# The bias of q, k and v in matmul rows that a column parity leaves empty, and the convolution's columns ordered by phase before channel

## The chip, the cores and the metric

The kernel runs on 1 core of one Trainium2 chip. The metric is the device time of one launch in microseconds (us). Before the change the median of 3 runs is 811.29 us (810.05 to 811.31). The core has TensorE (PE in the profile; PEld is its weight load), VectorE (DVE), ScalarE (ACT), GpSimd (POOL) and SyncE (SP), which here only issues DMAs.

## What is computed

The input x is (4, 32, 128, 128). Cut to what matters here:

```python
xw = group_norm(x) in windows of 16 x 16      # 64 windows an image
q = shuffle_invert(conv3(xw, qw, qb), 2)      # 3x3, 32 -> 32 channels, zero padding at the window's edge
k = shuffle_invert(conv3(xw, kw, kb), 2)      # a window's 16 x 16 pixels become 64 tokens
v = shuffle_invert(conv3(xw, vw, vb), 2)      # of 128 features: 32 channels x 2 x 2 phases
q, k, v = ln(q, gq, bq), ln(k, gk, bk), ln(v, gv, bv)
attn = softmax(q @ k.T * SCALE + bias[None])  # 8 heads of 16 features
out = (attn @ v) @ proj_w.T + proj_b          # back to pixels, plus xw: xr
y = xr + conv3(gelu(conv3(xr, c1w, c1b)), c2w, c2b)
return x + y
```

## The kernel before

Work is tiled by image (4), in an image by row of windows (8) and in a row by pair of windows (4): 32 pairs an image, 128 in all. One pair gives 128 tokens, the partitions of the result y_ps, which has 384 columns: 128 for q, 128 for k, 128 for v.

**The convolution of a pair** (PE, function step, lines 1010 and 1015) is one accumulation of 13 products in one bank. The input lies in SBUF as four copies shifted by one column: partition 32*col + channel, col 0 to 3. The free side is split by row parity, so one product covers one of four row offsets a (0 to 3) for both phases of the output. A phase (py, px) is the parity of the output pixel's row and column. Offset 0 is needed only by py = 0 and offset 3 only by py = 1, so these take half the columns (192). Input and weights are each a sum of two fp16 parts, high and low, and three products of them are taken: x_hi w_hi, x_hi w_lo, x_lo w_hi. The tokens' side is the stationary operand, the weights are streamed. Ahead of the twelve stands the bias product (line 1010): rows of ones (ones_b) against the bias split into three bf16 parts in b_parts. Since kx = col - px, columns of px = 0 have zero weights in rows 96 to 127 (col 3), and columns of px = 1 in rows 0 to 31 (col 0).

**Column order.** In each of q, k, v the 128 columns run over (py, head, channel in head, px). Normalising (ScalarE, line 855 for q and k, line 863 for v) reads them into the order (head, py, channel and px), so in runs of 8.

**The pipeline.** step(i) runs on each engine for i from -5 to 36 in an image. In step i the pair i+5 is convolved, the pair i+3 transposed (line 1040), the pair i scored (line 1056), i-2 has its softmax result transposed (line 1069) and i-3 is multiplied by v (line 1081). Each engine goes through its list in the order written, and semaphores tie them. From step 28 on PE also does the tiles of the first late convolution (c1, line 982), and the steps -5 to 2 of the next image do the second (c2, line 1138). After pair i+5's convolution VectorE takes the layer norm's statistics (line 541), GpSimd makes scales of them (lines 726 to 738), ScalarE normalises. The convolution of pair m waits for ln_v of pair m-2, which empties its bank.

**A row of inputs.** SP loads the shifted rows into xs (row, line 310), ScalarE normalises them (line 785), VectorE zeroes the window's edge, ScalarE writes x_hi (line 793, two halves; for row r in steps 4r-9 and 4r-8) and GpSimd x_lo (line 708). The row's first convolution is in step 4r-5.

**SP's order** in an image: the loads of rows 4 to 7 (each waits until the row two before it is normalised), the eight loads of xf, the four of the next image's xst, the next image's rows 0 to 3, then eight stores, each of which waits for its result. Image 0's rows 0 to 3 and the constants come ahead.

**Start.** VectorE finds the largest weights, scales, splits the weights (line 393) and takes the group norm's statistics (line 450). GpSimd splits the bias in nine operations (lines 694 to 696) and then takes the group norm's inverse deviation (line 701), on which the first row's normalisation waits.

Of the kernel before, what the change touches and what calls it, by code (L numbers as in the profile page):

```python
# [8 lines left out]
F16 = mybir.dt.float16  # L9
BF16 = mybir.dt.bfloat16  # L10
# [5 lines left out]
P = 128  # L16
# [4 lines left out]
E = 4 * C  # L21
# [17 lines left out]
W_TOP = 16.0  # L39
F16_TOP = 60000.0  # L40
# [4 lines left out]
GQ, BQ, GK, BK, GV, BV, PB, C1B, EVEN, ODD, C2B, EVEN2, ODD2, WIN0, WIN1, GVP, GVP1, BVP, BVP1 = range(19)  # L45
NVEC = 19
# [8 lines left out]
def conv_attention(nc, x_al, x_sh, wqkv, bqkv, bias_t, proj_t, vecs, w1, w2, ident, sel_mean, sel_ones, out):  # L55
    with ExitStack() as ctx:
# [22 lines left out]
        ones_f = sb("ones_f", [P, P])  # L79
        ones_b = sb("ones_b", [P, P], BF16)  # L80
# [4 lines left out]
        b_parts = sb("b_parts", [P, QKV], BF16)  # L85
        b_tmp = sb("b_tmp", [P, QKV], BF16)
# [84 lines left out]
        bias_split = sem("bias_split")  # L171
        c_scaled = sem("c_scaled")
# [80 lines left out]
        def by_head(y):  # L253

            return y.rearrange("p (y h x) -> p h y x", y=2, h=HEADS)
# [34 lines left out]
        def _(sp):  # L290
# [3 lines left out]
            for dst, src in ((wst, wqkv), (vec, vecs), (idf, ident), (bst, bqkv), (ones_f, sel_ones),  # L294
                             (selm, sel_mean)):
                load(dst, src, loaded_qkv)
# [15 lines left out]

            def image(b, followed):
                for r in range(4, NROW):
                    row(b, r)
# [3 lines left out]
                if followed:  # L319

                    sp.wait_ge(xr_begun, b * 4 + 5)
                    load_image(b + 1)
                    for r in range(4):
                        row(b + 1, r)
                for t in range(T2N):
                    sp.wait_ge(y_ready, b * T2N + (t + 1) + 1)
                    sp.dma_start(out[b, :, 512 * t:512 * (t + 1)], xf[t][:, :]).then_inc(stored, 16)
# [6 lines left out]
            for r in range(2, 4):  # L334
                row(0, r)
# [4 lines left out]
        def _(v):  # L340
# [29 lines left out]
            v.wait_ge(loaded_qkv, 16 * 6)  # L370
# [5 lines left out]
            v.tensor_copy(ones_b[:, :], ones_f[:, :])  # L376
            spread(0, 0, A_PROJ)

            link(v.tensor_scalar(sw[:, :], amax_all[:, 0:3], 1e-15, None, ALU.max))
# [287 lines left out]
        def _(pool):  # L667
# [12 lines left out]
            pool.wait_ge(loaded_qkv, 16 * 6)  # L680
# [12 lines left out]
            for j in range(3):  # L693
                bias_link(pool.tensor_copy(b_tmp[:, :], bst[:, :]))
                bias_link(pool.tensor_copy(b_parts[32 * j:32 * j + 32, :], b_tmp[32 * j:32 * j + 32, :]))
                bias_link(pool.tensor_tensor(bst[:, :], bst[:, :], b_tmp[:, :], ALU.subtract))
# [74 lines left out]
        def _(act):  # L771
# [48 lines left out]
            def step(i, p0, h0, r0, rr0, row0, b=None, followed=False, last=None):  # L820
# [27 lines left out]
                if has(i + 5):  # L848
# [5 lines left out]
                    for t in range(2):  # L854
                        ins = act.activation(qk_n[j][:, t, :].rearrange("p (h y x) -> p h y x", h=HEADS, y=2),  # L855
# [6 lines left out]
                    for w in range(2):  # L862
                        ins = act.activation(  # L863
                            v_bd[m % 8][:, :, w, 0:2 * HD].rearrange("p h (a y x) -> p h a y x", a=2, y=2),
                            y_ps[j][:, 2 * E:3 * E].rearrange("p (y h a x) -> p h a y x", y=2, h=HP, a=2),
# [69 lines left out]
        def _(pe):  # L935
# [62 lines left out]
            def step(i, p0, h0, r0, rr0, row0, b=None, followed=False, last=None):  # L998

                if has(i + 5):  # L1000
# [9 lines left out]
                    pe.matmul(y, ones_b[0:96, :], b_parts[0:96, :], start=True, stop=False)  # L1010
                    for a in range(4):

                        cols = {0: slice(0, E // 2), 3: slice(E // 2, E)}.get(a, slice(0, E))
                        for xx, ww in ((x_hi, w_hi), (x_hi, w_lo), (x_lo, w_hi)):
                            ins = pe.matmul(y.rearrange("p (t e) -> p t e", t=3)[:, :, cols],  # L1015
                                            xx[r % 2][:, s, a % 2, 2 * TS * (a // 2):2 * TS * (a // 2 + TS)],
                                            ww[:, a, :].rearrange("p (t e) -> p t e", t=3)[:, :, cols],
# [259 lines left out]
```

## Time and profile before

| | us |
|---|---|
| median of 3 runs | 811.29 |
| the profiled execution's own time | 810.2 |
| its span | 808.4 |
| PE matmul busy | 744.3 |
| PE weight loads busy (overlap the matmuls) | 549.4 |
| VectorE busy | 657.2 |
| ScalarE busy | 569.1 |
| GpSimd busy | 491.9 |

TensorE's granted clock is at 0.9 of full speed or more in each fortieth of the span. Busy time counts the durations of instructions; matmuls overlap, so what one costs is read from the distance between starts. A wait is put down to the instruction that came last. The chain of waits is the path that ended last, followed back to the start. Times in the rows below count from the span's start.

### The profile page before, as it was taken

How to read it: one execution, taken by the hardware profiler on the slowest of the kernel's cores; microseconds unless marked ns; L12 is line 12 of the kernel's file. 1: busy time of each engine (PE TensorE's matmuls, PEld its weight loads, DVE VectorE, ACT ScalarE, POOL GpSimd, SP SyncE). 2: the span in 40 equal slices, each digit the busy share in tenths (PEclk: the TensorE clock that was granted, in tenths of full speed). 3: DMA queues.
4: the chain of work that ended last, by engine and by line, in shares of the span. 5: the costliest groups of instructions: out<-in, count | busy, mean ns of one | idle time of the engine just before them, and what ended most of it. 6: DMA issues, size and time to landing. Idle time of an engine off the chain costs nothing.

```text
span 808.4 us, 18167 instructions
## 1 busy us (share of the span) xinstructions
PE 744.3 (92%) x5898; PEld 549.4 (68%) x5898; DVE 657.2 (81%) x2150; ACT 569.1 (70%) x1191; POOL 491.9 (61%) x1041
## 2 busy tenths in 40 slices
PE   0469999999899999999899999999999999999988
PEld 0247877777556778877555778777655688787753
DVE  6549889897859899897967989899775989887675
ACT  1399888767367988876547978876737788878630
POOL 6368778741457788763346777874244778886210
PEclk9999999999999999999999999999999999999999
DMA  7112331000013161000101332100101314000002
GB/s 266 59 30 60 96 144 60 2 1 23 38 65 97 33 239 44 18 1 1 59 33 54 110 125 116 60 1 2 56 5 66 98 32 135 2 2 2 2 1 104
DMA packets 17662, 47.32 MB, mean 59 GB/s; under 512 B 2080, under 2 KB 2720, under 8 KB 17568
## 3 DMA queue, kind: packets, MB, share of 16 engines
q1 hardware_dynamic: 17568, 46.15, 16.7%
q8 instruction: 48, 0.79, 0.4%
q14 instruction: 46, 0.38, 0.1%
HBM read 37.76 MB, written 8.39 MB: 57 GB/s over the span
## 4 chain that ended last, share of the span: by engine, by line
PE 67%; DVE 12%; ACT 9%; issue 5%; POOL 5%; DMA 0%; SPq 0%; POOLq 0%; ACTq 0%; DVEq 0%
PE y_ps L1015 18%; PE o_bank L1081 9%; PE s_ps L1056 8%; PE pt_ps L1069 7%; PE y_ps L982 4%; PE s_ps L1097 3%; PE t_ps L1040 3%; PE ox_ps L1138 3%; PE o_bank L1138 3%; PE pt_ps L1138 3%; PE s_ps L1138 3%; PE y_ps L1010 2%; DVE h_lo L505 2%; DVE h_hi L502 2%; ACT qk_n L855 1%
## 5 line engine op out<-in xcount | busy, mean ns | idle before, releaser
L743 POOL TENSOR_TENSOR sc<-sc,mx 128x512 f32<-128x512 f32 x128 | 133.7, 1044 | 59.9 <-DVE mx L568 59.9
L855 ACT ACTIVATE qk_n<-y_ps,ln_nr,ln_rs 128x128 f32<-128x128 f32 x256 | 104.4, 464 | 88.4 <-POOL ln_nr L733 88.2
L1015 PE MATMUL y_ps<-w_hi,x_hi 128*128 128x192 f16 (+1 forms) x512 | 147.2, 287 | 0.0
L1015 PE MATMUL y_ps<-w_hi,x_lo 128*128 128x192 f16 (+1 forms) x512 | 146.9, 287 | 0.0
L1015 PE MATMUL y_ps<-w_lo,x_hi 128*128 128x192 f16 (+1 forms) x512 | 146.7, 287 | 0.0
L541 DVE BATCH_NORM_STATS2 ln_st<-y_ps 128x6 f32<-128x128 f32 x384 | 88.8, 287 | 60.1 <-PE y_ps L1015 58.9
L1081 PE MATMUL o_bank<-v_bd,pt 128*128 128x66 f32 x1024 | 129.1, 269 | 3.9 <-DVE on L589 3.8
L1081 PEld LDWEIGHTS o_bank<-v_bd,pt 128*128 128x128 f32 x1024 | 124.4, 192 | 5.5 <-DVE pt L575 4.7
L730 POOL TENSOR_TENSOR ln_rs<-ln_ve,neg_half 128x3 f32<-128x3 f32 x128 | 113.4, 886 | 10.7
L870 ACT ACTIVATE sc<-sc 128x512 f32<-128x512 f32 x128 | 82.8, 647 | 39.3 <-POOL sc L743 39.3
L863 ACT ACTIVATE v_bd<-y_ps,ln_vs 128x128 f32<-128x128 f32 x256 | 105.2, 475 | 0.0
L726 POOL TENSOR_TENSOR ln_ve<-ln_mv,eps_y 128x3 f32<-128x3 f32 x128 | 35.2, 275 | 105.6 <-DVE ln_mv L546 105.6
L561 DVE TENSOR_TENSOR sc<-s_ps,biasS 128x512 f32<-128x512 f32 x128 | 85.2, 666 | 16.6 <-PE s_ps L1056 16.5
L1056 PE MATMUL s_ps<-k_m,q_m 64*128 64x128 f32 x1024 | 91.6, 297 | 0.0
L568 DVE TENSOR_REDUCE mx<-sc 128x8 f32<-128x512 f32 x128 | 87.9, 686 | 4.4
L575 DVE COPY pt<-pt_ps 128x512 f32<-128x512 f32 x128 | 87.2, 681 | 2.8 <-PE pt_ps L1069 2.6
L715 POOL TENSOR_TENSOR xr_lo<-xr,xr_hi 128x512 f16<-128x512 f32 x32 | 36.2, 1131 | 86.8 <-ACT xr_hi L811 86.8
L1069 PE MATMUL pt_ps<-idf,sc 128*128 128x128 f32 x512 | 83.5, 286 | 0.0
L1056 PEld LDWEIGHTS s_ps<-k_m,q_m 64*128 64x128 f32 x1024 | 67.0, 186 | 22.8 <-issue 22.8
L589 DVE TENSOR_TENSOR on<-o_bank,rs 64x128 f32<-64x128 f32 x256 | 73.9, 289 | 6.2
L708 POOL TENSOR_TENSOR x_lo<-xnf,x_hi 128x512 f16<-128x512 f32 x64 | 76.1, 1196 | 3.7 <-ACT x_hi L793 3.7
L840 ACT ACTIVATE q_m<-t_ps,q_aff 128x256 f32<-128x256 f32 x128 | 66.1, 579 | 14.5 <-PE t_ps L1040 14.5
(190 smaller groups left out, 1607.7 us busy)
## 6 DMA issues: line engine op xcount, KB each, us to landing
xs<-in_x_sh_dram SPq DMA_DIRECT2D x32, 576.0 KB, 4.4
xst<-in_x_al_dram SPq DMA_DIRECT2D x16, 512.0 KB, 8.2
xf<-in_x_al_dram SPq DMA_DIRECT2D x32, 256.0 KB, 5.2
out_dram<-xf SPq DMA_DIRECT2D x32, 256.0 KB, 2.0
wst<-in_wqkv_dram SPq DMA_DIRECT2D x1, 768.0 KB, 4.2
w1s<-in_w_dram SPq DMA_DIRECT2D x1, 256.0 KB, 8.7
w2s<-in_w_dram SPq DMA_DIRECT2D x1, 256.0 KB, 8.7
biasS<-in_bias_t_dram SPq DMA_DIRECT2D x1, 256.0 KB, 9.6
```

The lines of the kernel that those rows point to most:

```text
L541: ins = v.bn_stats(ln_st[m % 2][:, t, :], y_ps[m % 2][:, E * t:E * (t + 1)])
L568: v.tensor_reduce(mx[i % 2][:, :, :], sc[i % 4][:, :, :, :].rearrange("p h k w -> p h w k"), AX.X, ALU.max).then_inc(maxed, 1)
L575: v.tensor_copy(pt[m % 2][:, :, :], pt_ps[:, :, :]).then_inc(pt_copied, 1)
L730: pool.tensor_tensor(ln_rs[j][:, :], ln_ve[j][:, :], neg_half[:, 0:3], ALU.pow).then_inc(ln_pow, 1)
L743: pool.tensor_tensor(sc[i % 4][:, :, :, :], sc[i % 4][:, :, :, :], mx[i % 2][:, :, :].unsqueeze(2).to_broadcast([P, HP, TOK, 2]), ALU.subt ...
L855: ins = act.activation(qk_n[j][:, t, :].rearrange("p (h y x) -> p h y x", h=HEADS, y=2), by_head(y_ps[j][:, E * t:E * (t + 1)]), ACT.Identity,
L863: ins = act.activation(v_bd[m % 8][:, :, w, 0:2 * HD].rearrange("p h (a y x) -> p h a y x", a=2, y=2), y_ps[j][:, 2 * E:3 * E].rearrange(" ...
L1015: ins = pe.matmul(y.rearrange("p (t e) -> p t e", t=3)[:, :, cols], xx[r % 2][:, s, a % 2, 2 * TS * (a // 2):2 * TS * (a // 2 + TS)], ww[: ...
L1056: ins = pe.matmul(out[:, :, :, w], q_m[h % 2][rows, i % 2, w, :, :].rearrange("p a t -> p (a t)"), k_m[h % 2][rows, i % 2, w, :, :], start ...
L1069: ins = pe.transpose(pt_ps[:, g, :], sc[m % 4][:, g, :, :].rearrange("p k w -> p (k w)"), idf[:, :])
L1081: ins = pe.matmul(o_ps[:, g, :, :].rearrange("p w d -> p (w d)"), pt[m % 2][:, g, :], v_bd[m % 8][:, g, :, :].rearrange("p w d -> p (w d)" ...
L1138: ins = pe.matmul(c2_bank[t], ww[:, a, :], hh[:, T2R * t + ay:T2R * (t + 1) + ay, ax:ax + G], start=(a == 0 and n == 0), stop=(a == 3 and ...
```

## The change

The bias product goes. A second copy of the row's input, x_u, is kept for each of two rows in turn: for each column parity x it holds 96 partitions of x_hi at the odd row parity (the ones with weights for that parity), copied by a DMA on SP's queue, and in the other 32 partitions constants, 4096, 1, 1/1024 and zeros, filled once at the start by GpSimd. w_b holds the high weights of row offset 1, the 192 columns of each parity together, and in the rows that the parity leaves empty the three fp16 parts of the bias, each divided by its constant. The product x_hi w_hi of offset 1 becomes two products of 192 columns, x_u against w_b, which stand last; the others come in the order of offsets 2, 0, 3, 1. The columns now run over (py, px, head, channel in head), and normalising reads runs of 4. The bias's largest value now bounds the weights' scale as well, and the bias is split on GpSimd by 18 operations instead of nine. SP's queue gets two copies a row, each pair waiting for x_hi, and the order of its loads and stores changes. The input sel_ones is gone.

```diff
+B_STEPS = (4096.0, 1.0, 1.0 / 1024)
+B_REL = 2.0 ** -16
...
-        b_parts = sb("b_parts", [P, QKV], BF16)
-        b_tmp = sb("b_tmp", [P, QKV], BF16)
+        b_part = [sb(f"b_part{j}", [P, QKV], F16) for j in range(3)]
+        b_tmp = sb("b_tmp", [P, QKV])
+        b_max = sb("b_max", [P, 3])
+        w_b = sb("w_b", [P, 2, QKV // 2], F16)
+        x_u = [sb(f"x_u{i}", [P, 2, NPAIR, P], F16) for i in range(2)]
...
-            return y.rearrange("p (y h x) -> p h y x", y=2, h=HEADS)
+            return y.rearrange("p (y h c) -> p h y c", y=4, h=HEADS)
...
+            def with_bias_rows(b, r):
+
+                sp.wait_ge(xhi_done, (b * NROW + r) * 2 + 2)
+                for x in range(2):
+                    rows = slice(32 * x, 32 * x + 96)
+                    sp.dma_start(x_u[r % 2][rows, x, :, :], x_hi[r % 2][rows, :, 1, 0:2 * TS * TS]).then_inc(
+                        loaded_u[r % 2], 16)
+
+            def store(b, t):
+                sp.wait_ge(y_ready, b * T2N + (t + 1) + 1)
+                sp.dma_start(out[b, :, 512 * t:512 * (t + 1)], xf[t][:, :]).then_inc(stored, 16)
+
             def image(b, followed):
-                for r in range(4, NROW):
-                    row(b, r)
+                for r in range(3, 6):
+                    row(b, r + 2)
+                    with_bias_rows(b, r)
                 sp.wait_ge(stored, b * (T2N * 16) + 16)
                 for t in range(T2N):
                     sp.dma_start(xf[t][:, :], x_al[b, :, 512 * t:512 * (t + 1)]).then_inc(xf_loaded, 16)
@@ -320,19 +337,32 @@
 
                     sp.wait_ge(xr_begun, b * 4 + 5)
                     load_image(b + 1)
-                    for r in range(4):
+                with_bias_rows(b, 6)
+                with_bias_rows(b, 7)
+                if followed:
+                    for r in range(2):
                         row(b + 1, r)
-                for t in range(T2N):
-                    sp.wait_ge(y_ready, b * T2N + (t + 1) + 1)
-                    sp.dma_start(out[b, :, 512 * t:512 * (t + 1)], xf[t][:, :]).then_inc(stored, 16)
+                    for r in range(2):
+                        with_bias_rows(b + 1, r)
+                        row(b + 1, r + 2)
+                for t in range(5):
+                    store(b, t)
+                if followed:
+                    row(b + 1, 4)
+                    with_bias_rows(b + 1, 2)
+                for t in range(5, T2N):
+                    store(b, t)
 
             load_image(0)
             for r in range(2):
                 row(0, r)
             for dst, src in ((projw, proj_t), (w1s, w1), (w2s, w2), (biasS, bias_t)):
                 load(dst, src, loaded_consts)
-            for r in range(2, 4):
-                row(0, r)
+            for r in range(2):
+                with_bias_rows(0, r)
+                row(0, r + 2)
+            row(0, 4)
+            with_bias_rows(0, 2)
             images(image)
...
-            v.tensor_copy(ones_b[:, :], ones_f[:, :])
+            v.tensor_reduce(b_max[:, :], bst[:, :].rearrange("p (t e) -> p t e", t=3), AX.X, ALU.max,
+                            apply_absolute_value=True).then_inc(b_maxed, 1)
             spread(0, 0, A_PROJ)
 
-            link(v.tensor_scalar(sw[:, :], amax_all[:, 0:3], 1e-15, None, ALU.max))
+            v.wait_ge(b_maxed, 1)
+            link(v.scalar_tensor_tensor(sw[:, :], b_max[:, :], B_REL, amax_all[:, 0:3], ALU.mult, ALU.max))
+            link(v.tensor_scalar(sw[:, :], sw[:, :], 1e-15, None, ALU.max))
...
-            for j in range(3):
-                bias_link(pool.tensor_copy(b_tmp[:, :], bst[:, :]))
-                bias_link(pool.tensor_copy(b_parts[32 * j:32 * j + 32, :], b_tmp[32 * j:32 * j + 32, :]))
-                bias_link(pool.tensor_tensor(bst[:, :], bst[:, :], b_tmp[:, :], ALU.subtract))
+            bias_link(pool.tensor_scalar(b_part[0][:, :], bst[:, :], 1.0 / B_STEPS[0], None, ALU.mult))
+            bias_link(pool.tensor_scalar(b_tmp[:, :], b_part[0][:, :], B_STEPS[0], None, ALU.mult))
+            bias_link(pool.tensor_tensor(bst[:, :], bst[:, :], b_tmp[:, :], ALU.subtract))
+            bias_link(pool.tensor_copy(b_part[1][:, :], bst[:, :]))
+            bias_link(pool.tensor_tensor(bst[:, :], bst[:, :], b_part[1][:, :], ALU.subtract))
+            bias_link(pool.tensor_scalar(b_part[2][:, :], bst[:, :], 1.0 / B_STEPS[2], None, ALU.mult))
+            pool.wait_ge(w_hi_done, 3)
+            by_phase = lambda t: t.rearrange("p (n x c) -> p x n c", n=6, x=2)
+            for x in range(2):
+                bias_link(pool.tensor_copy(w_b[:, x, :].rearrange("p (n c) -> p n c", n=6), by_phase(w_hi[:, 1, :])[:, x, :, :]))
+            for j in (2, 1, 0):
+                for x in range(2):
+                    rows = slice(96 * (1 - x), 96 * (1 - x) + j + 1)
+                    bias_link(pool.tensor_copy(w_b[rows, x, :].rearrange("p (n c) -> p n c", n=6),
+                                               by_phase(b_part[j][:, :])[rows, x, :, :]))
+            for t in x_u:
+                for x in range(2):
+                    rows = slice(96 * (1 - x), 96 * (1 - x) + 32)
+                    bias_link(pool.tensor_copy(t[rows, x, :, :].rearrange("p m t -> p (m t)"),
+                                               vec[rows, BROW:BROW + 1].to_broadcast([32, NPAIR * P])))
...
-                        ins = act.activation(qk_n[j][:, t, :].rearrange("p (h y x) -> p h y x", h=HEADS, y=2),
+                        ins = act.activation(qk_n[j][:, t, :].rearrange("p (h y c) -> p h y c", h=HEADS, y=4),
...
-                            v_bd[m % 8][:, :, w, 0:2 * HD].rearrange("p h (a y x) -> p h a y x", a=2, y=2),
-                            y_ps[j][:, 2 * E:3 * E].rearrange("p (y h a x) -> p h a y x", y=2, h=HP, a=2),
+                            v_bd[m % 8][:, :, w, 0:2 * HD].rearrange("p h (a y c) -> p h a y c", a=2, y=4),
+                            y_ps[j][:, 2 * E:3 * E].rearrange("p (y h a c) -> p h a y c", y=4, h=HP, a=2),
...
-                    pe.matmul(y, ones_b[0:96, :], b_parts[0:96, :], start=True, stop=False)
-                    for a in range(4):
+                    for a in (2, 0, 3, 1):
 
                         cols = {0: slice(0, E // 2), 3: slice(E // 2, E)}.get(a, slice(0, E))
-                        for xx, ww in ((x_hi, w_hi), (x_hi, w_lo), (x_lo, w_hi)):
-                            ins = pe.matmul(y.rearrange("p (t e) -> p t e", t=3)[:, :, cols],
-                                            xx[r % 2][:, s, a % 2, 2 * TS * (a // 2):2 * TS * (a // 2 + TS)],
-                                            ww[:, a, :].rearrange("p (t e) -> p t e", t=3)[:, :, cols],
-                                            start=False, stop=(a == 3 and xx is x_lo))
+                        for xx, ww in ((x_hi, w_hi), (x_hi, w_lo), (x_lo, w_hi))[a == 1:]:
+                            pe.matmul(y.rearrange("p (t e) -> p t e", t=3)[:, :, cols],
+                                      xx[r % 2][:, s, a % 2, 2 * TS * (a // 2):2 * TS * (a // 2 + TS)],
+                                      ww[:, a, :].rearrange("p (t e) -> p t e", t=3)[:, :, cols],
+                                      start=(a == 2 and ww is w_hi and xx is x_hi), stop=False)
+                    if s == 0:
+                        pe.wait_ge(loaded_u[r % 2], 32 * (rr0 + r // 2 + 1))
+                    for x in range(2):
+                        ins = pe.matmul(y.rearrange("p (n x c) -> p x n c", n=6, x=2)[:, x, :, :],
+                                        x_u[r % 2][:, x, s, :], w_b[:, x, :].rearrange("p (n c) -> p n c", n=6),
+                                        start=False, stop=x == 1)
                     ins.then_inc(conv_done, 1)
...
-            pe.wait_ge(bias_split, 9)
+            pe.wait_ge(bias_split, 18)
...
-    hd, py, c4, px = np.unravel_index(e, (HEADS, 2, HD // 4, 2))
+    hd, py, px, c4 = np.unravel_index(e, (HEADS, 2, 2, HD // 4))
     f_nat = (hd * (HD // 4) + c4) * 4 + py * 2 + px
 
-    py, hd, c4, px = np.unravel_index(e, (2, HEADS, HD // 4, 2))
+    py, px, hd, c4 = np.unravel_index(e, (2, 2, HEADS, HD // 4))
```

## Rows read from the trace of the kernel before

**Rows 1.** The page: busy time by engine; the chain of waits, shares by line.

```profile
PE 744.3 (92%) x5898; PEld 549.4 (68%) x5898; DVE 657.2 (81%) x2150; ACT 569.1 (70%) x1191; POOL 491.9 (61%) x1041
...
PE y_ps L1015 18%; PE o_bank L1081 9%; PE s_ps L1056 8%; PE pt_ps L1069 7%; PE y_ps L982 4%; PE s_ps L1097 3%; PE t_ps L1040 3%; PE ox_ps L1138 3%; PE o_bank L1138 3%; PE pt_ps L1138 3%; PE s_ps L1138 3%; PE y_ps L1010 2%; DVE h_lo L505 2%; DVE h_hi L502 2%; ACT qk_n L855 1%
```

**Rows 2.** Busy us by stretch: length, PE, PEld, DVE, ACT, POOL, clock, DMA share, GB/s.

```profile
50.00:75.00 25.00, 20.90 (x178) 15.48 (x179) 18.90 (x68) 25.00 (x52) 19.60 (x47) 1.00 0.09 26
75.00:146.00 71.00, 71.00 (x623) 56.76 (x622) 63.85 (x225) 59.53 (x133) 58.15 (x128) 1.00 0.28 94
100.72:118.06 17.34, 17.34 (x154) 13.89 (x152) 15.59 (x56) 15.03 (x33) 14.43 (x32) 1.00 0.45 174
```

**Rows 3.** The chain in order of time, a plain step: start, us, what.

```profile
101.05 1.47 PE y_ps L1015 x12
```

**Rows 4.** The same chain where it leaves and regains TensorE, image 0.

```profile
146.48 0.70 DVE ln_st L541 x3
...
212.89 1.86 PE y_ps L982 x12
```

**Rows 5.** PE's timeline, one convolution's first products; a group of its weight loads.

```profile
109.97 0.33 PE L1010 MATMUL y_ps<-b_parts,ones_b 96*128 96x384 bf16 x1
110.14 0.25 PE L1015 MATMUL y_ps<-w_hi,x_hi 128*128 128x192 f16 x1
110.22 0.24 PE L1015 MATMUL y_ps<-w_lo,x_hi 128*128 128x192 f16 x1
...
110.39 0.33 PE L1015 MATMUL y_ps<-w_hi,x_hi 128*128 128x384 f16 x1
110.55 0.33 PE L1015 MATMUL y_ps<-w_lo,x_hi 128*128 128x384 f16 x1
...
L1015 PEld LDWEIGHTS y_ps<-w_lo,x_hi 128*128 128x128 f16 x512 | 50.3, 98 | 25.5 <-issue 0.7
```

**Rows 6.** VectorE: a group in 100.72 to 118.06 us; its waits in 75 to 200.

```profile
L541 DVE BATCH_NORM_STATS2 ln_st<-y_ps 128x6 f32<-128x128 f32 x12 | 2.8, 286 | 1.1 <-PE y_ps L1015 1.1
...
DVE ln_st L541 <- PE y_ps L1015: 5.8, 15, 0.6
```

**Rows 7.** ScalarE's groups, whole kernel: busy us, mean ns | idle before.

```profile
L863 ACT ACTIVATE v_bd<-y_ps,ln_vs 128x128 f32<-128x128 f32 x256 | 105.2, 475 | 0.0
L855 ACT ACTIVATE qk_n<-y_ps,ln_nr,ln_rs 128x128 f32<-128x128 f32 x256 | 104.4, 464 | 88.4 <-POOL ln_nr L733 88.2
...
L840 ACT ACTIVATE q_m<-t_ps,q_aff 128x256 f32<-128x256 f32 x128 | 66.1, 579 | 14.5 <-PE t_ps L1040 14.5
```

**Rows 8.** Timelines of SP's queue, VectorE and GpSimd at the start.

```profile
2.57 0.43 SPq L292 DMA_DIRECT2D ones_f<-in_sel_ones_dram  x1
...
9.24 0.28 DVE L363 TENSOR_REDUCE top<-t_ps 11x1 f32<-11x128 f32 x1 [0.42 <-PE t_ps L940]
...
28.70 0.68 DVE L409 TENSOR_REDUCE amax<-w1s 128x1 f32<-128x512 f32 x1
...
12.30 0.50 POOL L694 CAST b_tmp<-bst 128x384 bf16<-128x384 f32 x1 [4.36 <-DVE bst L386]
...
13.44 0.92 POOL L696 TENSOR_TENSOR bst<-bst,b_tmp 128x384 f32<-128x384 f32 x1
14.42 0.85 POOL L694 CAST b_tmp<-bst 128x384 bf16<-128x384 f32 x1
...
24.21 0.55 POOL L701 TENSOR_TENSOR gm<-gm,neg_half 128x1 f32<-128x1 f32 x1 [4.60 <-DVE gm L472]
```

**Rows 9.** A row's x_hi and first convolution (timelines); the DMA queue and stores (page).

```profile
104.28 0.64 ACT L793 ACTIVATE x_hi<-xnf 128x512 f16<-128x512 f32 x1
...
114.02 0.33 PE L1010 MATMUL y_ps<-b_parts,ones_b 96*128 96x384 bf16 x1
...
q1 hardware_dynamic: 17568, 46.15, 16.7%
...
out_dram<-xf SPq DMA_DIRECT2D x32, 256.0 KB, 2.0
```

More of the change, by code:

```diff
@@ L42 @@
 GN_BOUND = float(IMG)
-GQ, BQ, GK, BK, GV, BV, PB, C1B, EVEN, ODD, C2B, EVEN2, ODD2, WIN0, WIN1, GVP, GVP1, BVP, BVP1 = range(19)
-NVEC = 19
+GQ, BQ, GK, BK, GV, BV, PB, C1B, EVEN, ODD, C2B, EVEN2, ODD2, WIN0, WIN1, GVP, GVP1, BVP, BVP1, BROW = range(20)
+NVEC = 20
 T1R = 5
@@ L52, with conv_attention @@
 T2N = G // T2R
-def conv_attention(nc, x_al, x_sh, wqkv, bqkv, bias_t, proj_t, vecs, w1, w2, ident, sel_mean, sel_ones, out):
+def conv_attention(nc, x_al, x_sh, wqkv, bqkv, bias_t, proj_t, vecs, w1, w2, ident, sel_mean, out):
     with ExitStack() as ctx:
@@ L78, in conv_attention @@
         selm = sb("selm", [P, P])
-        ones_f = sb("ones_f", [P, P])
-        ones_b = sb("ones_b", [P, P], BF16)
         wst = sb("wst", [P, 4, QKV])
@@ L171, in conv_attention @@
         bias_split = sem("bias_split")
+        b_maxed = sem("b_maxed")
+        loaded_u = [sem(f"loaded_u{i}") for i in range(2)]
         c_scaled = sem("c_scaled")
@@ L292, in load @@
                 sp.dma_start(dst[tuple(slice(None) for _ in dst.shape)], src).then_inc(done, 16)
-            for dst, src in ((wst, wqkv), (vec, vecs), (idf, ident), (bst, bqkv), (ones_f, sel_ones),
-                             (selm, sel_mean)):
+            for dst, src in ((wst, wqkv), (vec, vecs), (idf, ident), (bst, bqkv), (selm, sel_mean)):
                 load(dst, src, loaded_qkv)
@@ L368, in spread @@
                 link(v.tensor_copy(amax_all[:, lo:hi], t_ps[:, 0, 0, 0:hi - lo]))
-            v.wait_ge(loaded_qkv, 16 * 6)
+            v.wait_ge(loaded_qkv, 16 * 5)
             for t in range(3):
@@ L679, in _ @@
             pool.wait_ge(zeroed, 1)
-            pool.wait_ge(loaded_qkv, 16 * 6)
+            pool.wait_ge(loaded_qkv, 16 * 5)
             for t in v_bd:
@@ L1151, in image @@
                         c2(b, t)
-            pe.wait_ge(loaded_qkv, 16 * 6)
+            pe.wait_ge(loaded_qkv, 16 * 5)
             spread(0, 0, A_PROJ)
@@ L1268, in _lay_out @@
                      g["proj_b"][e_m], g["c1b"][e_ph[2]], even, 1 - even, g["c2b"][e_ph[2]], even2, 1 - even2, first, 1 - first,
-                     *by_par[0], *by_par[1]], axis=1)
+                     *by_par[0], *by_par[1], np.tile([*B_STEPS] + [0.0] * (C - 3), 4).astype(np.float32)], axis=1)
     ident = np.eye(P, dtype=np.float32)
     sel_mean = (e[:, None] % C == e[None, :] % C).astype(np.float32) / 4
-    sel_ones = np.zeros((P, P), np.float32)
-    sel_ones[[0, 32, 64]] = 1.0
     arrays = dict(x_al=x_al, x_sh=x_sh, wqkv=wqkv, bqkv=bqkv, bias_t=bias_t, proj_t=proj_t, vecs=vecs,
-                  w1=w1, w2=w2, ident=ident, sel_mean=sel_mean, sel_ones=sel_ones)
+                  w1=w1, w2=w2, ident=ident, sel_mean=sel_mean)
     return {k: np.ascontiguousarray(v) for k, v in arrays.items()}, None
```

## The prediction

> **What bounds the kernel now.** I read the page first [rows 1]. TensorE's matmuls are busy for 744.3 of 808.4 us, VectorE for 657.2, and the chain of work that ended last puts 18% of the span on line 1015 (the twelve input products of a convolution) and 2% on line 1010 (the bias product). Busy shares are averages over unlike stages, so next come the busy times by stretch [rows 2]: from 75 to 146 us of image 0 TensorE is busy for 71.00 of 71.00 us, from 50 to 75 us ScalarE for 25.00 of 25.00. A row of four window pairs, from 100.72 to 118.06 us, takes 17.34 us, all of it TensorE's. The chain in order of time says the same: there it goes from one TensorE piece to the next, the twelve products of a pair as one piece of 1.47 us [rows 3]. It leaves TensorE in three kinds of places: at the start of image 0, where ScalarE carries it [rows 2]; at 146.48 us, step 22, when VectorE also has the next image's statistics; and in the change of images, from 186 us until it is back on TensorE for good at 212.89 [rows 4], where no convolution stands on it. Images 1 to 3 repeat the last two.
>
> How much of the convolution is on the chain: 18% of 808.4 us is 145.5 us, and the twelve products take 1.47 us a pair [rows 3], so 99 of the 128 pairs, 25 an image.
>
> **TensorE, per pair.** Today there are 13 products: one of 384 columns over the bias rows, six of 384 and six of 192. Starts, not durations, give the cost, since matmuls overlap [rows 5]: the bias product starts at 109.97, the next at 110.14; products of 192 columns start 0.08 us apart, of 384 columns 0.16 us. After the change there are 13 again, five of 384 and eight of 192: the bias product goes, and the 384-column product of x_hi and w_hi for row offset 1 becomes two halves by column parity. In columns 3840 become 3456. The removed product is 0.17 by its start, 0.16 by its columns [rows 5]; the split is 2 x 0.08 - 0.16 = 0. I take a saving of 0.163 us a pair, 20.9 us over 128, and on the 99 of the chain 16.1 us.
>
> Could the split cost something? Two ways. First, weight loads: each lasts 98 ns [rows 5], more than the 82 ns of a 192-column product, and now six such products stand in a row where three stood. In the three the starts are still 0.08 apart, so the loads overlap; if they did not in a longer row, eight products would lose 16 ns each, 0.13 us a pair. I take 0. Second, the result is written in six runs of 32 columns, 64 apart. The 192-column products of today write three runs of 64, 128 apart, and take half of a 384-column product's time [rows 5], so gaps as such are free; I take 0 and keep double time, +0.16 us a pair, as the other end. The Trainium skill speaks against the change here: "PSUM — Partial Sum Buffer", Specifications, says that any non-contiguous access pattern slows matmuls significantly. Rows 5 do not agree with it for runs of 64; by it the halves would cost about what the bias product did. It is a rival below.
>
> **What takes over.** VectorE waits 1.1 us per row for the convolution [rows 6]. The row becomes 4 x 0.163 = 0.65 us shorter, so 0.45 us are left: TensorE stays the bound in plain rows. From step 22 on VectorE has the statistics too, and the chain already passes to it at step 22 [rows 4]. With 0.163 us less per step it will pass over three or four steps earlier, and at the two ends of image 0's ScalarE stretch likewise. I take 14 of the 99 pairs, 2.2 us. Ends: 0 pairs (nothing lost), and half of what is saved in plain rows, 8 us, if the 0.45 us are eaten by order and latency.
>
> **ScalarE and the new column order.** Normalising q, k and v now reads and writes runs of 4 elements, not 8. Line 855 takes 464 ns for 128 elements, line 840 takes 579 ns for 256 that it reads one by one, two apart [rows 7]. Short runs show no price: I take 0. The upper end is what a change of pattern has ever shown here, 11 ns (475 against 464, lines 863 and 855), 4 x 11 ns a step; ScalarE's 15.0 us in a row of 17.34 [rows 2] hide it, except in the stretch that ScalarE bounds, from 50 us on [rows 2], some 9 steps, 0.4 us. Below zero: nothing gets fewer elements, so no gain.
>
> **The start.** VectorE: the cast of the ones becomes an absolute maximum over 384 bias columns, an estimate of 0.5 us from 0.68 us for 512, and most of it lies in the cast's time and the 0.42 us in which VectorE then waits for TensorE [rows 8]; one more tiny operation is 0.2 us on the path. One DMA of 64 KB less in front saves its issue, 0.43 us [rows 8]. Sum -0.2 us.
>
> GpSimd splits the bias before it inverts the group norm's deviation, which the first row's normalisation needs. Today nine operations run from 12.30 to 19.61 us, the inverse starts at 24.21 after 4.60 us of idle time [rows 8]. Now there are eighteen, each waiting for the one before, 0.06 to 0.07 us apart. One-input operations on 384 columns take 0.50, and 0.85 at 14.42, when VectorE splits the weights; two-input ones take 0.92 [rows 8], and I add the same 0.35 beside VectorE. Six of them: 0.57 + 0.57 + 1.34 + 0.92 + 1.34 + 0.57 = 5.3 us. Eight copies of 192 columns, halved to 0.3 and the gap: 3.0. Four fills of 512 columns by 0.50 x 512/384 = 0.67 and the gap: 3.0. Together 11.3 us from 12.3, so 23.6: 0.6 us before the inverse. I take 0; the ends are 0 and +2 us (all copies at 0.5 us, conversions slower), since a delay there moves the whole kernel. By the Trainium skill ("GPSIMD Engine Reference", Elementwise — side-by-side cycle accounting) 512 elements of a one-input operation take 769 ns; the four fills would then be 0.4 us longer, and the end 24.0, still hidden.
>
> **The copied tiles.** Every row now has two DMAs on SP's queue that copy 96 partitions of x_hi into x_u, with its constants in the other 32. They are issued when ScalarE has written x_hi (line 793, start 104.28, 0.64 long) and needed at the end of the first convolution of that row, which starts at 114.02: its last two products at about 115.5, 10.6 us later, 10.1 in shorter steps [rows 9]. Cost of the two: issues of 0.43 us each [rows 8]; landing of a 256 KB store is 2.0 us [rows 9]. Their 96 x 4 x 2 = 768 pieces of 256 bytes are a size that the trace hardly has. Lower end: by bytes, under 1 us. Upper end: each piece costs as much as a mean packet of 2.6 KB, 16.7% x 808.4 x 16 / 17568 = 123 ns [rows 9], so 5.9 us on 16 engines; 0.9 + 2.0 + 5.9 = 8.8 us, still before 10.1. I take 4 us and no stall. What SP's order queues behind the new waits: row 5's copies stand ahead of the loads xf and xst, which move from step 9 to step 12, some 4.2 MB or 24 us at the 174 GB/s seen [rows 2], and are used at steps 21 and 22, nine steps of 4.2 us later. Row 6's copies, issued at step 16, stand behind what is left of them and are needed at step 19. Row 4 of the next image is now issued before the last three stores, not after them, and the result tile of a store is reused an image later. None of this is late. The first row of image 0 has the least room; what it may cost is in the 2 us of the start.
>
> **Sum.** Against the profiled execution's own 810.2 us (span 808.4, 1.8 around it): -16.1 + 2.2 - 0.2 = -14.1, so 796.1 us. The median of the runs is 811.3, 1.1 above it; on that scale **797 us**, -1.7%.
>
> **Rivals.**
> (a) Another engine becomes the bound in plain rows as well: VectorE's 0.45 us of slack is spent by GpSimd's chain of tiny operations and ScalarE's fixed order. Half the saving is left, 803 us. For: VectorE's waits in 75 to 200 us are 5.8 us over 15 waits only [rows 6]. Against: the slack stays positive per row. 0.14.
> (b) The split product costs time, by its runs of 32 or by weight loads: 0.13 to 0.16 us a pair on 99, 13 to 16 us back, 810 us. Against: rows 5. 0.05.
> (c) Slower than before: the copies land late. The place is the last two products of every row's first convolution. Every us beyond 10.1 stands on TensorE 31 times; it decides from 0.5 us late on (16 us), a landing 10.6 us after x_hi. At 1 us late: 797 + 31 = 828 us. For: pieces of 256 bytes, and other loads in the same queues. Against: even mean packets give 8.8 us. 0.05.
> (d) Nothing new takes over and the ramp gains too: 99 pairs or all 128, 795 down to 790. Against: rows 4, where the chain passes to VectorE already. 0.05.
> (e) GpSimd's chain overruns by 2 us: 799, within the range; part of the forecast's chance, 0.71.
>
> **How the numbers follow.** A measurement of this kernel can tell 0.2%, 1.6 us, from no change. The range is 792 to 804: the forecast with its ends (0 to 4 us lost to takeovers, 0 to 2 at the start) and rival (a). Faster: forecast, (a) and (d), 0.90; same: most of (b), 0.04; slower: (c) and a rest of (b), 0.06.
>
> **What would show it.** TensorE: 5 x 384 and 8 x 192 columns a pair, no line with b_parts, 1.47 us from first to last start, and a plain row in 16.7 us. If it shows 17.3 with gaps on TensorE, the step on takeovers fell; if starts of the split halves are over 0.1 us apart, that on the split. In TensorE's waits a DMA of x_u, 32 times, would be rival (c). GpSimd's inverse starting right after the fills and later than 24.2 shows the start mis-sized. VectorE's waits per row should fall to near 0.45 us. I am wrong altogether if TensorE's busy time falls by 21 us and the span by under 8.

## The result, and the profile after

| | before | changed |
|---|---|---|
| median, us | 811.30 (4 runs, 810.05 to 812.55) | 798.07 (4 runs, 796.51 to 799.20) |
| ratio to before | | 0.9836, 95% interval 0.9809 to 0.9862 |
| the profiled execution's own time | 810.2 | 796.94 |
| its span | 808.4 | 795.1 |

The change makes the kernel 13.2 us faster; 797 was forecast. Two runs in this document lie far off all others, 1115.49 and 3756.38 us, both of e9 below; they are left out of its ratio, and its trace, of the first of them with TensorE's clock at 0.57, is not read.

Busy time on the page of the changed kernel stands against [rows 1], its DMA queue against [rows 9]; the last line is the new copies on SP's queue (KB each, us to landing):

```profile
PE 726.6 (91%) x5898; PEld 546.7 (69%) x5898; DVE 658.6 (83%) x2151; ACT 568.5 (71%) x1191; POOL 495.2 (62%) x1050
...
q1 hardware_dynamic: 43024, 52.39, 21.1%
...
x_u<-x_hi SPq DMA_DIRECT2D x64, 96.0 KB, 2.3
```

TensorE lost 17.7 us of busy time with the same 5898 products, less than the 20.9 us of 128 pairs. Part of the difference is one convolution at half the clock (next section): e6, whose trace has it at the full clock, lost 21.1. Another part is that this figure moves by itself: e3, with the products of the kernel before, has 742.2 us against 744.3. No other engine's busy time moved by over 4 us. The queue carries 25456 packets more, nearly all of them the copies' small pieces, and the DMA share rises by 4 points only. A copy lands after 2.3 us.

One convolution of the changed kernel in PE's timeline, columns as in [rows 5]:

```profile
110.39 0.33 PE L1063 MATMUL y_ps<-w_hi,x_hi 128*128 128x384 f16 x1
...
110.88 0.25 PE L1063 MATMUL y_ps<-w_hi,x_hi 128*128 128x192 f16 x1
110.96 0.25 PE L1063 MATMUL y_ps<-w_lo,x_hi 128*128 128x192 f16 x1
111.05 0.25 PE L1063 MATMUL y_ps<-w_hi,x_lo 128*128 128x192 f16 x1
...
111.70 0.33 PE L1070 MATMUL y_ps<-w_b,x_u 128*128 128x192 f16 x2
111.87 0.38 PE L1094 MATMUL t_ps<-idf,qk_n 128*128 128x128 f32 x2
```

Here the first start and the transposes' start give the whole: 1.48 us, where the bias product and the twelve took 1.64. All six products of 192 columns in a row (three are shown) start 0.08 apart, and the two halves together take 0.17, what one product of 384 takes.

A plain row in the busy times by stretch, against [rows 2], and VectorE's group in a plain row, against [rows 6]:

```profile
100.10:116.80 16.70, 16.70 (x153) 13.72 (x153) 15.57 (x55) 14.51 (x33) 14.23 (x31) 1.00 0.53 166
```

```profile
L574 DVE BATCH_NORM_STATS2 ln_st<-y_ps 128x6 f32<-128x128 f32 x12 | 2.8, 286 | 0.6 <-PE y_ps L1070 0.5
```

TensorE still fills the row, and VectorE waits 0.5 us for the convolution where it waited 1.1.

To see where the 13.3 us of span come from, I set the end of each pair's convolution in one trace against the other (before: start of the bias product + 1.64; changed: start of the halves + 0.165). Pairs count from 0 in each image, so pair 2 is the third convolution. The changed kernel's lead in us:

```
image 0: pair 3  -1.80   pair 9  -1.52   pair 28  +1.10   pair 29 +0.74   pair 31  +1.25
image 1: pair 0  +1.50   pair 1  +1.28   pair 28  +5.09   pair 29 +4.73   pair 31  +5.26
image 2: pair 0  +5.27                   pair 28  +9.03   pair 29 +8.67   pair 31  +9.19
image 3: pair 0  +9.58                   pair 28 +13.12   pair 29 +12.77  pair 31 +13.42
```

By pair 3 it is 1.80 us behind. It wins back only some 0.3 us of that up to pair 11, in the stretch that ScalarE bounds, and then gains 0.16 us in most pairs, with small steps back at pair 29 and at an image's second pair: 15.2 us from pair 3 to the end.

### The profile page after: what moved, and what is told of

It reads as the page before. It is cut to its first block, busy times and chain, and to the rows that moved or that the text cites. A ratio compares the mean times of both kernels' runs of the same rounds, so it can differ in the third digit from the quotient of the medians.

```text
span 795.1 us, 18242 instructions
## 1 busy us (share of the span) xinstructions
PE 726.6 (91%) x5898; PEld 546.7 (69%) x5898; DVE 658.6 (83%) x2151; ACT 568.5 (71%) x1191; POOL 495.2 (62%) x1050
## 3 DMA queue, kind: packets, MB, share of 16 engines
q1 hardware_dynamic: 43024, 52.39, 21.1%
## 4 chain that ended last, share of the span: by engine, by line
PE 63%; DVE 13%; ACT 9%; POOL 7%; issue 6%; DMA 0%; SPq 0%; POOLq 0%; ACTq 0%; DVEq 0%
PE y_ps L1063 15%; PE o_bank L1135 9%; PE s_ps L1110 8%; PE pt_ps L1123 6%; PE y_ps L1031 4%; PE s_ps L1151 3%; PE t_ps L1094 3%; PE s_ps L1192 3%; PE pt_ps L1192 3%; PE ox_ps L1192 2%; PE o_bank L1192 2%; DVE h_lo L538 2%; PE y_ps L1070 2%; DVE h_hi L535 2%; POOL ln_rs L779 2%
## 5 line engine op out<-in xcount | busy, mean ns | idle before, releaser
L1063 PE MATMUL y_ps<-w_hi,x_lo 128*128 128x384 f16 (+1 forms) x512 | 148.0, 289 | 0.0
L1063 PE MATMUL y_ps<-w_lo,x_hi 128*128 128x384 f16 (+1 forms) x512 | 138.0, 290 | 0.0
L1063 PE MATMUL y_ps<-w_hi,x_hi 128*128 128x192 f16 (+1 forms) x384 | 106.4, 277 | 7.4 <-ACT v_bd L912 7.0
L594 DVE TENSOR_TENSOR sc<-s_ps,biasS 128x512 f32<-128x512 f32 x128 | 85.2, 666 | 16.8 <-PE s_ps L1110 16.4
```

The lines of the kernel that those rows point to most:

```text
L594: v.tensor_tensor(sc[i % 4][:, :, :, :].rearrange("p (a h) k w -> p a (h k w)", a=2), s_ps[:, :, 0:256], biasS[:, :, :], ALU.add).then_inc ...
```

## Why it started late

GpSimd's timeline at the start, which answers to [rows 8]:

```profile
11.73 1.20 POOL L726 TENSOR_SCALAR b_part<-bst 128x384 f16<-128x384 f32 x1 [4.61 <-DVE bst L419]
13.02 1.17 POOL L727 TENSOR_SCALAR b_tmp<-b_part 128x384 f32<-128x384 f16 x1
14.27 1.30 POOL L728 TENSOR_TENSOR bst<-bst,b_tmp 128x384 f32<-128x384 f32 x1
...
17.57 1.17 POOL L731 TENSOR_SCALAR b_part<-bst 128x384 f16<-128x384 f32 x1
18.80 0.75 POOL L735 COPY w_b<-w_hi 128x192 f16<-128x192 f16 x2
19.61 2.35 POOL L739 COPY w_b<-b_part 3x192 f16<-3x192 f16 x6
22.03 2.62 POOL L744 CAST x_u<-vec 32x512 f16<-32x512 f32 x4
24.73 0.57 POOL L750 TENSOR_TENSOR gm<-gm,neg_half 128x1 f32<-128x1 f32 x1
```

The inverse (line 750) follows the fills without idle time, 0.52 us later than before although the chain began 0.57 earlier. The chain of waits of the changed kernel, followed through its start, goes from one of these operations to the next from 11.73 to 25.3 us; before, it went through VectorE there. The first convolution starts at 32.92 us, 0.54 later than before. The copies and fills cost what was estimated (6.0 us for both; they took 5.9, from 18.80 to 24.66, gaps within; a fill 0.61 where 0.67 was put), but the three products with a constant take 1.17 to 1.20 us, not the 0.50 of a cast.

The rest of the 1.8 us, some 1.2, is TensorE's clock. Busy times by stretch around the third convolution, before and changed (the columns of [rows 2]; the clock is the third from the end):

```profile
40.70:42.40 1.70, 1.65 (x14) 1.20 (x15) 0.00 (x0) 1.30 (x4) 0.59 (x4) 1.00 0.00 0
```

```profile
38.30:41.30 3.00, 0.14 (x3) 0.02 (x2) 1.07 (x7) 1.51 (x4) 2.75 (x8) 0.99 0.00 0
41.30:44.30 3.00, 3.00 (x14) 2.09 (x15) 0.00 (x0) 2.68 (x5) 0.52 (x4) 0.50 0.00 0
```

After some 3 us with nothing to do, TensorE did this convolution at 1.2 GHz in the changed kernel, its products of 384 columns 0.32 us apart, and at 2.4 GHz in the kernel before, after the same kind of wait (3.15 us there, 2.86 here). It stands on the chain; 1.2 us went there. The column of the clock has to be read beside the starts: from 32.4 to 36 us the trace of the kernel before gives it as 1.00 too, yet the first convolution's products of 384 columns start 0.32 us apart, at half the clock, in both traces.

## The experiments

All were timed in rounds beside the kernel before, whose median moved between 810.89 and 811.34 us from one group of rounds to another. So a difference of two changed kernels from different groups is better read from their ratios, and one under 2 us is hardly more than the spread. Edits are cut to their main lines.

**e1_no_bias**, from the kernel before:

```diff
-                    pe.matmul(y, ones_b[0:96, :], b_parts[0:96, :], start=True, stop=False)
-                    for a in range(4):
+                    for a in (2, 0, 3, 1):
```

> The kernel before without its bias product (the bias is left out of q, k, v; the twelve products in the order of offsets 2, 0, 3, 1); no x_u, no copies, the start and SP's order as before. Theory A (the change gains by TensorE's 384 columns alone, 0.163 us on some 92 pairs, and lost 1.6 us at the start, by GpSimd's chain and the clock at the third convolution): 811.3 - 15.0 = 796.3 us, faster than the changed kernel by 1 to 2. Rival B (a part of the gain comes from SP's new order, earlier loads or the column order): 800 us or more.

Measured: 795.14 us, ratio 0.9804 (0.9790 to 0.9817). The removed columns alone account for 16 us; the changed kernel's other parts cost 2 to 3 us net. Rival B falls.

**e2_one_more**, from the changed kernel:

```diff
+                    pe.matmul(y.rearrange("p (t e) -> p t e", t=3)[:, :, :],
+                              x_lo[r % 2][:, s, 0, 2 * TS:2 * TS * (1 + TS)],
+                              w_lo[:, 2, :].rearrange("p (t e) -> p t e", t=3)[:, :, :], start=False, stop=False)
```

> The changed kernel with one more product of 384 columns in each convolution (x_lo w_lo of offset 2), so 3840 columns as before; all else as changed. Theory A: the gain goes back, 798.1 + 15.0 = 813 us, slower than before by the 1.6 us of the start. Rival B: under 808 us. Rival C (the copies and SP's waits cost something that the gain hides): over 816 us.

Measured: 812.34 us, ratio 1.0015 (1.0006 to 1.0024). With the columns back the gain is gone, and 1 us more. So nothing of it came from SP's order, unless the copies cost as much as the order gave; together with the start they cost 1 us net.

**e3_order_only**, from the kernel before:

```diff
-            return y.rearrange("p (y h x) -> p h y x", y=2, h=HEADS)
+            return y.rearrange("p (y h c) -> p h y c", y=4, h=HEADS)
...
-    py, hd, c4, px = np.unravel_index(e, (2, HEADS, HD // 4, 2))
+    py, px, hd, c4 = np.unravel_index(e, (2, 2, HEADS, HD // 4))
```

> The kernel before with only the column order changed (phase, then channel), so that ScalarE reads and writes runs of 4 for 8. Theory A: 811.3 us within 0.2%, lines 855 and 863 at 464 and 475 ns within 5 ns. Rival (short runs cost ScalarE time): 4 x 11 ns a step, 0.4 to 2 us slower, with longer ACTIVATEs.

Measured: 811.23 us, ratio 0.9996 (0.9987 to 1.0005). ScalarE's groups in its trace, against [rows 7]:

```profile
L863 ACT ACTIVATE v_bd<-y_ps,ln_vs 128x128 f32<-128x128 f32 x256 | 105.2, 475 | 0.0
L855 ACT ACTIVATE qk_n<-y_ps,ln_nr,ln_rs 128x128 f32<-128x128 f32 x256 | 104.4, 464 | 88.4 <-POOL ln_nr L733 88.2
```

Runs of 4 cost what runs of 8 do, to the nanosecond.

**e4_four_copies**, from the changed kernel:

```diff
+                for n in range(3):
+                    for x in range(2):
+                        rows = slice(32 * x, 32 * x + 96)
+                        sp.dma_start(x_v[r % 2][rows, n, x, :, :], x_hi[r % 2][rows, :, 1, 0:2 * TS * TS]).then_inc(
+                            loaded_u[r % 2], 16)
...
-                        pe.wait_ge(loaded_u[r % 2], 32 * (rr0 + r // 2 + 1))
+                        pe.wait_ge(loaded_u[r % 2], 128 * (rr0 + r // 2 + 1))
```

> The changed kernel with three further copies of the same pieces into a spare tile ahead of each row's own, eight DMAs a row in place of two; TensorE waits for all. Issues of 0.62 us make 5.0 us, the last lands some 7.5 to 8 us after x_hi, before the 10 us at which it is needed. Theory A (copies have slack): 798 us within 0.3%, no wait of TensorE for a DMA. Rival C (the copies are near the limit, or SP's queue holds up loads and stores): TensorE waits in each row's first convolution, 2 us a row, 850 us.

Measured: 796.77 us, ratio 0.9833 (0.9813 to 0.9853). TensorE's waits in its trace (us in total, times, longest) have one for these DMAs, in image 0's first row, where the room is least:

```profile
PE y_ps L1076 <- DMA x_u<-x_hi: 1.0, 1, 1.0
```

The changed kernel has no such wait. Rival (c) of the prediction is far off: four times the copies are hidden too, but for this 1 us in the first row.

**e5_two_less**, from the changed kernel:

```diff
-                        for xx, ww in ((x_hi, w_hi), (x_hi, w_lo), (x_lo, w_hi))[a == 1:]:
+                        for xx, ww in ((x_hi, w_hi), (x_hi, w_lo), (x_lo, w_hi))[a == 1:1 if a == 2 else 3]:
```

> The changed kernel without x_hi w_lo and x_lo w_hi of row offset 2 (left out of q, k and v): 768 columns less, 0.326 us a pair. Theory A (in plain rows VectorE now has only 0.5 us of waiting a row left, so it becomes the bound; beside the late convolution at an image's start TensorE stays the bound): 0.5 us of 1.3 in each of some 5 rows an image, 0.33 us on 9 pairs in images 1 to 3: 2.5 x 4 + 2.9 x 3 = 19 us, 779 us, and TensorE with idle time in plain rows. Rival (TensorE stays the bound everywhere that it is now): 92 x 0.326 = 30 us, 768 us.

Measured: 792.26 us, ratio 0.9782 (0.9761 to 0.9804). 42 us of TensorE's work left out give 6 by the medians and 4.4 by the ratios. Not 19 either: theory A was right that another bound takes over, but put it 0.5 us a row too low. A plain row of e5 against the same of the changed kernel above:

```profile
100.77:117.42 16.65, 15.44 (x140) 12.47 (x138) 15.72 (x55) 14.46 (x33) 13.83 (x32) 1.00 0.50 157
```

TensorE is idle for 1.2 us and the row as long as before, 16.65 for 16.70. The chain of e5 from 280 to 320 us runs through GpSimd for more than half (line 779 alone 17.8%); in the changed kernel it runs through TensorE alone there. What e5 gains it gains elsewhere: by the distance between convolutions, pairs 4 to 8 of images 1 to 3 take 18.7 us for 20.0 and pairs 12 to 16 take 16.2 for 16.7, while from pair 16 on four pairs take 16.7 to 16.9 in both. In e5's trace the clock in image 0's start is lower, 0.82 on average from 50 to 75 us, where its lead over the changed kernel goes from -0.2 (pair 3) to -2.3 us (pair 8). It loses another 3.4 us of lead, 5.2 to 1.8, between the last pair of image 2 and the first of image 3; the cause of that is open.

**e6_fills_on_act**, from the changed kernel: the eight copies into w_b and the four fills of x_u become ScalarE's, behind its weights.

```diff
-                    bias_link(pool.tensor_copy(t[rows, x, :, :].rearrange("p m t -> p (m t)"),
-                                               vec[rows, BROW:BROW + 1].to_broadcast([32, NPAIR * P])))
+                    u_link(act.activation(t[rows, x, :, :].rearrange("p m t -> p (m t)"),
+                                          vec[rows, BROW:BROW + 1].to_broadcast([32, NPAIR * P]), ACT.Copy))
```

> The changed kernel with the eight copies into w_b and the four fills of x_u on ScalarE, which is idle at the start, and only the six splits on GpSimd. Theory A (GpSimd's chain holds up the group norm's inverse): the inverse starts at 24.1 us again or earlier, not 24.7, the first convolution some 0.6 to 1 us earlier; 797.3 us median, with the profile's convolution 0 at 32.3 or below. Rival (the start is bound by VectorE alone): no convolution earlier than 32.9, 798.1.

Measured: 796.07 us, ratio 0.9824 (0.9807 to 0.9841). GpSimd's inverse in its timeline:

```profile
23.67 0.58 POOL L737 TENSOR_TENSOR gm<-gm,neg_half 128x1 f32<-128x1 f32 x1 [4.88 <-DVE gm L506]
```

It starts 1.06 us earlier than in the changed kernel, with 4.88 us of idle time ahead of it again, and the first convolution also starts 1.06 us earlier, at 31.86. So GpSimd's overrun cost the changed kernel 1.06 us. The medians' 2.0 us (1.0 by the ratios) are within both kernels' spread, so how much of them is this and how much the clock is not told apart by times.

**e7_filler**, from the changed kernel: 16 products whose result nobody uses, in TensorE's wait before the third convolution; **e8_both** is e6 and e7 together.

```diff
+                if b == 0 and last is None and i + 5 == 2:
+                    for _ in range(16):
+                        pe.matmul(ox_ps[:, 0:QKV], x_hi[0][:, 0, 0, 0:2 * TS * TS], w_hi[:, 0, :], start=True, stop=True)
```

> The changed kernel with 16 products of 384 columns into a free bank between the second and the third convolution of image 0, in the 3 us in which TensorE waits for ScalarE. Theory A (the third convolution ran at 1.2 GHz after that wait, 3.0 us where 1.5 would do): its products start 0.16 us apart and the kernel is 1 to 1.5 us faster where it was slow, 796.9 median, with less spread. Rival (the clock at that point does not hang on this wait, or the filler runs into the convolution): no change or 0.5 us slower.

> Both of the last two in one kernel: 795.5 to 796.5 us if both hold, 2 us below the changed kernel; near the 795.1 us of the kernel without bias.

Measured: e7 796.55 us, ratio 0.9829 (0.9816 to 0.9842), its five runs within 1.7 us; e8 794.86 us, ratio 0.9805 (0.9792 to 0.9819), its four runs within 0.3 us. The third convolution of e8 by stretch:

```profile
40.10:41.60 1.50, 1.50 (x14) 1.05 (x12) 0.00 (x0) 0.98 (x4) 0.80 (x4) 1.00 0.00 0
```

1.50 us at the full clock, where the changed kernel's trace had 3.0. Against the changed kernel, e8's convolutions end 1.04 us earlier at pair 0 and 2.34 us earlier at pair 3, and the lead stays at 2.4 us to the end: the two losses of the start, GpSimd's and the clock's, are what e8 wins back, and nothing else.

That the filler secured the clock is not shown. Of the traces without a filler, those of the kernel before, e1, e2, e3, e4 and e6 have the third convolution at the full clock too, after waits of 1.7 to 3.9 us, and those of the changed kernel, e5, e11 and e12 have it at half, after waits of 2.9 to 3.7 us: the wait alone does not tell which it will be. In e1 the fourth was slow instead (0.50 from 42.4 to 45.0 us), and in e10 below, which has the filler, later ones were. I have one trace of each kernel. e8 is complete, the fastest complete kernel of the study, 3.2 us below the changed one by the medians (2.5 by the ratios), and level with e1, which has no bias at all.

**e9_two_less_xr_later** and its repeat **e12**, from e5; **e10**, from e8:

```diff
+        low_split_in = {14: (0,), 18: (1,), 22: (2,), 26: (3,), 30: (4,), 31: (5,), 33: (6,)}
...
-                for r in split_in.get(i, ()):
+                for r in low_split_in.get(i, ()):
```

> e5_two_less with one change of GpSimd's order: the low part of xr (line 764) is taken in steps 14, 18, 22, 26, 30 and not in 11, 15, 19, 23, 27, where GpSimd stands idle for 1.35 us in each row until ScalarE has its high part. Theory A (GpSimd's queue, with that wait in it, is what bounds a plain row of e5 at 16.65 us): the wait goes, a plain row falls to VectorE's 16.1 us, and 5 rows an image by 0.5 us make 10 us, 782 us. Rival (VectorE bounds the row already): 792 us, a row of 16.6 us.

> e8_both (complete and fastest so far, 794.86 us) with the same move of line 764. A plain row is TensorE's there (16.7 us), so it stays; what can gain is the last rows of an image, where the chain leaves TensorE. Theory A: 0 to 3 us faster, 792 to 795 us. Rival (the low part of xr comes too late for the late convolution): 1 us slower or more.

> e9_two_less_xr_later once more, for a profile with an undisturbed TensorE clock. Its times say 791.5 to 796, no gain over e5. Theory A (the 1.35 us wait of GpSimd in a row was the bound): plain rows of 16.1 us. Rival B (the wait only hides time that GpSimd has over; the bound is its two steps with line 757 and the chain into VectorE and ScalarE): plain rows of 16.5 us or more.

**e11_two_less_light_low**, from e5:

```diff
+            for t in x_lo:
+                pool.memset(t[:, 1:NPAIR, 0, 2 * TS:2 * TS * HALF], 0.0)
+                pool.memset(t[:, 1:NPAIR, 1, 0:2 * TS * TS], 0.0)
...
-                pool.tensor_tensor(rows_of(x_lo[r % 2], z), rows_of(xnf[r % 2], z), rows_of(x_hi[r % 2], z),
+                pool.tensor_tensor(rows_of(x_lo[r % 2], z)[:, 0:1, :], rows_of(xnf[r % 2], z)[:, 0:1, :], rows_of(x_hi[r % 2], z)[:, 0:1, :],
```

> e5_two_less with GpSimd's low part of x (line 757) taken for one of four pairs in a row (the others are zero and left out of q, k and v): 0.8 us less on GpSimd in two of four steps, its order kept. Theory A (in e5 a plain row of 16.7 us is bound by GpSimd's list, which is full in the two steps with line 757): a plain row falls to about 16.1 us, where VectorE is the bound, 5 rows an image by 0.5 us: 782 us. Rival (VectorE bounds it at 16.7 already): rows of 16.6 us, 792 us.

Measured: e9 ratio 0.9793 (0.9773 to 0.9812), the same as e5. e12: 794.80 us, ratio 0.9791 (0.9760 to 0.9822). e11: 784.71 us, ratio 0.9667 (0.9651 to 0.9683). e10: 799.19 us, ratio 0.9844 (0.9829 to 0.9860). Two stretches of two rows and a bit, of e11 and then of e12:

```profile
300.00:338.00 38.00, 35.63 (x331) 29.50 (x329) 36.15 (x124) 32.38 (x74) 29.42 (x71) 1.00 0.36 122
```

```profile
300.00:338.00 38.00, 35.70 (x328) 29.50 (x327) 35.85 (x127) 31.49 (x73) 32.31 (x72) 1.00 0.26 87
```

The theory that GpSimd's list bounds e5's plain row falls: with 3.4 us less of GpSimd's work in the stretch (e11), and with its 1.35 us wait gone (e12), the distance between two rows' first convolutions from pair 16 of an image on stays 16.5 to 16.8 us in images 1 to 3. VectorE is busy for 36.15 of 38 us with small gaps between its 124 instructions. Asked for its waits from 300 to 338 us, the traces of e5 and e11 list none for VectorE, that of e12 0.7 us, that of the changed kernel 1.2. So VectorE fits as the bound; no run relieved it, so that is argued, not shown. e11 is 7.6 us faster than e5 all the same. Its trace is of the slowest of its six runs (789.27 us), only 2.6 us shorter than e5's, and puts nothing of that in these rows: 1.2 us of lead are there at the first convolution, and 4.0 come between images 2 and 3, where e5's trace had lost 3.4. What makes its other runs faster is open. e10, the move of line 764 in a complete kernel, is 4.3 us slower than e8 by the medians. The traces are 4.9 us apart. 0.6 us of that is there at the first convolution: the load of selm, the first thing VectorE waits for, landed after 4.01 us where e8's took 3.41, and the chain of waits passes it. 2.6 us more arise in image 0's start, where e10's clock was 0.57 from 48 to 52 us, 0.72 from 56 to 62 and 0.50 from 76 to 78, and e8's 1.00. Some 1.5 us come after it, two tenths at a time, at steps 16 and 20 of an image (just before pairs 22 and 26 are convolved), where TensorE waits 0.2 us for ScalarE's ot. TensorE's waits for the low part of xr are the same 6.1 us in both traces, so the reason that the rival gave is not it.

## Why the prediction was right

**TensorE, per pair: right.** 13 products, 3456 columns, 0.16 us less. Neither the runs of 32 nor the weight loads cost anything; six starts in a row stand 0.08 us apart. The Trainium skill ("PSUM — Partial Sum Buffer", Specifications) says that any non-contiguous access pattern slows matmuls significantly. The trace does not agree with it for runs of 32 columns of fp32, 64 apart: 0.17 us for the two halves, where rival (b) had put up to 0.16 us more.

**What takes over: right in kind, the size a little high.** 2.2 us were put down, 14 of 99 pairs. The lead grows by 15.2 us from pair 3 of image 0 to the end, 93 pairs' worth at 0.163, so 1 us is lost against 99. VectorE's wait per row was forecast at 0.45 and is 0.5.

**ScalarE and the column order: right**, 0 (e3).

**The copied tiles: right**, no stall. A landing of 2.3 us and an issue of 0.62 (0.43 was taken) put the last piece some 3.5 us after x_hi; e4 shows room for four times as much in all rows but the first.

**The start: mis-sized.** It was to gain 0.2 us and lost 1.8. GpSimd's chain was to end at 23.6 and ended at 24.66, since three products with a constant were priced as casts: 0.50 us against 1.17 to 1.20. By e6 this cost 1.06 us. That is rival (e) in a small form. The row for it was missing, the nearest taken, and its upper end, +2 us, held the loss. The clock of the third convolution, 1.2 us of the 1.8, was no term of the sum. The gain on VectorE and the missing load cannot be told from chance: without the overrun, in e6, the first convolution starts 0.52 us before that of the kernel before, but in e1, whose start has no change, it starts 0.38 us before it, since the load of selm, the first on the chain, landed sooner (3.30 us for 3.68).

The two errors, +1.3 on the lead's growth and -2.0 at the start, nearly cancel: the profiled execution was forecast at 796.1 and measured at 796.94. The mechanism was right; that the number is so close is in part luck. Rival (a) is the one that came nearest: e5 shows that the kernel now stands at that edge, where a further cut on TensorE is worth nothing in a row from pair 16 on.

## What to carry to other kernels

Rows or columns of a product that are zero by structure are free room for a constant term: the cost moves from a product per tile to a copy per row of tiles, which a queue with slack takes. Cost such a cut by starts, times the number of times that the chain of waits passes the line, and read beside it how long the next engine waits per round: here 1.1 us against 0.65 cut said that the whole cut would count in such a row, and that the next would not. Work moved to the start was on the path here, although the steady state never sees it: look for an idle engine, and price each operation by its own kind.

## What the runs showed that was not expected

- GpSimd took 1.17 to 1.20 us to multiply 384 columns by a constant, 0.50 to 0.85 to cast them, 0.91 to 1.30 to subtract two tiles. So here a product with a constant was as dear as a two-input operation.
- The few convolutions of image 0's start, with waits of 1 to 4 us between them, ran at either clock from one kernel's trace to the next, with and without a filler. Products of 384 columns stood 0.32 us apart in one and 0.17 in another. On the chain this came to 1.2 us in the changed kernel and to some 2.6 us in e10 against e8; e1's slow fourth convolution delayed the next by at most 0.2 us, since TensorE then waited 1.17 us where it waits 2.4 elsewhere. So before a difference of 1 to 3 us is put down to an edit, the clock of both starts has to be compared.
- The first load on which VectorE waits (selm) held the chain for 3.2 to 4.1 us in different traces: up to 0.9 us of difference between two traces come from there.
- 64 copies in pieces of 256 bytes from SBUF to SBUF landed in 2.3 us each for 96 KB (2.1 to 4.9), little over the 2.0 us of a 256 KB store in pieces of 2 KB.
